# A differential attention block: row maxima taken 1024 columns at a time, scores issued in pairs

## The reference, cut to what matters

```python
B, T, _ = x.shape                        # 4, 1024
q = apply_rope((x @ Wq).reshape(B, T, 32, 8))
k = apply_rope((x @ Wk).reshape(B, T, 16, 8))
v = (x @ Wv).reshape(B, T, 8, 2, 8)
...
def causal_attn(q, k, v, scale):
    s = jnp.einsum('bthd,bshd->bhts', q, k) * scale
    s = jnp.where(mask[None, None], s, jnp.finfo(s.dtype).min)
    p = jax.nn.softmax(s, axis=-1)
    return jnp.einsum('bhts,bshd->bthd', p, v)
attn = causal_attn(q1, k1, vcat, scale) - lambda_full * causal_attn(q2, k2, vcat, scale)
```

## Time and profile before

| | |
|---|---|
| median of 3 runs | 2000.56 us (1993.98 to 2002.34) |
| the profiled execution, span | 2000.2 us |
| PE busy | 1869.5 us, 93% |
| DVE busy | 1456.6 us, 73% |
| ACT busy | 1050.9 us, 53% |
| POOL busy | 670.8 us, 34% |
| first maximum to last value product | 123.3 to 1205.3 us |

### The profile page before, as it was taken

The page is one execution under the profiler, slowest core; times in us unless marked ns, Lnnn a source line. Parts: engine busy times, 40 slices in busy tenths (PEclk is TensorE's granted clock), DMA queues, the critical chain, the costliest instruction groups (busy, mean ns, idle before and its releaser), DMA issues. The chain is left out here.

```text
span 2000.2 us, 42093 instructions
## 1 busy us (share of the span) xinstructions
PE 1869.5 (93%) x11851; PEld 1116.7 (56%) x11851; DVE 1456.6 (73%) x3474; ACT 1050.9 (53%) x2538; POOL 670.8 (34%) x730
## 2 busy tenths in 40 slices
PE   7888999999999999999999999999899999999985
PEld 4543434444343444434444347777688888788874
DVE  7898888988888888888888854444367865433347
ACT  3325567676676666666666644344333323344445
POOL 4542441111111232322223213777703443133324
PEclk9877899999999999999999999999999999999998
DMA  4443342212222121212212102443322211354247
GB/s 129 138 144 103 99 114 71 71 25 71 59 63 80 46 62 40 65 41 59 55 45 62 42 15 85 124 124 111 111 74 88 74 51 54 111 170 141 86 159 150
DMA packets 196455, 170.42 MB, mean 85 GB/s; under 512 B 92120, under 2 KB 176392, under 8 KB 195976
## 3 DMA queue, kind: packets, MB, share of 16 engines
q1 hardware_dynamic: 173064, 115.75, 20.9%
q0 software_dynamic: 20128, 50.35, 8.0%
q10 hardware_dynamic: 3168, 3.15, 0.6%
HBM read 104.16 MB, written 76.90 MB: 91 GB/s over the span
## 5 line engine op out<-in xcount | busy, mean ns | idle before, releaser
L1768 DVE TENSOR_REDUCE mx<-ps 128x1 f32<-128x512 f32 (+3 forms) x1536 | 763.4, 549 | 106.1 <-PE ps L889 85.5
L1358 ACT ACTIVATE fbuf<-ps 128x512 f32<-128x512 f32 (+3 forms) x1024 | 459.4, 507 | 255.6 <-PE ps L900 251.3
L885 PE MATMUL ps<-rbuf 72*128 72x512 bf16 (+3 forms) x1536 | 505.2, 336 | 32.8 <-DVE mx L1768 19.9
L900 PE MATMUL ps<-rbuf 75*128 75x512 bf16 (+3 forms) x1536 | 500.8, 333 | 21.1 <-DMA rbuf<-mrows 18.3
L900 PEld LDWEIGHTS ps<-rbuf 75*128 75x128 bf16 x1536 | 150.3, 98 | 328.0 <-ACT fbuf L1358 138.0
L1358 ACT ACTIVATE gbuf<-ps 128x512 f32<-128x512 f32 (+2 forms) x512 | 211.3, 469 | 102.0 <-PE ps L900 100.9
L732 POOL TENSOR_SCALAR_AFFINE_SELECT gbuf<-gbuf 128x512 f32<-128x512 f32 x96 | 61.4, 640 | 530.3 <-ACT gbuf L1358 530.3
L885 PEld LDWEIGHTS ps<-rbuf 72*128 72x128 bf16 x1536 | 151.9, 99 | 146.3 <-DVE mx L1768 102.9
L915 PE MATMUL ps<-fbuf 128*32 128x512 f32 (+3 forms) x2048 | 228.8, 519 | 2.1 <-issue 0.2
L889 PE MATMUL ps<-maskq,identb 128*128 128x128 bf16 x1024 | 230.1, 225 | 0.0
L739 POOL DMA_INDIRECT y_scr<-wstage,bidx x138 | 138.8, 1006 | 242.2 <-ACT wstage L1402 218.9
(11 more groups left out here) (271 smaller groups left out, 2961.4 us busy)
## 6 DMA issues: line engine op xcount, KB each, us to landing
rbuf<-q_scr SPq DMA_DIRECT2D x192, 96.0 KB
xs_scr<-in_pad SPq DMA_DIRECT2D x8, 1360.0 KB, 6.4
gbuf<-xs_scr SPq DMA_DIRECT2D x69, 136.0 KB, 2.2
gbuf<-xe_scr SPq DMA_DIRECT2D x69, 136.0 KB, 2.1
rbuf<-k_scr SPq DMA_DIRECT2D x192, 48.0 KB
gbuf<-y_scr SPq DMA_DIRECT2D x8, 1024.0 KB, 5.3
q_scr<-gbuf SPq DMA_DIRECT2D x48, 128.0 KB
gbuf<-a_scr SPq DMA_DIRECT2D x12, 512.0 KB, 4.7
```

Source lines behind the costliest of these rows:

```text
L885: ins = pe.matmul(o, qst[par][0:PROWS, i // 4, m, P * (i % 4):P * (i % 4 + 1)], kst[par][0:PROWS, m % 2, 512 * piece:512 * piece + width], ...
L900: pe.matmul(o, kst[par][0:SROWS, m % 2, P * j:P * (j + 1)], qst[par][0:SROWS, h, m, t0:C], start=True, stop=True).then_inc(b_scores, 1)
L1358: act.activation(prob(s)[:, t0:C], ps[:, s % SRING, t0:C], ACT.Exp, scale=SCALE).then_inc(b_exp, 1)
L1768: dve.tensor_reduce(mx[:, i // 4, piece, n:n + 1], ps[:, SRING + s % SRING, 0:width], AX, ALU.max, negate=True).then_inc(b_maxed, 1)
```

## The change: what it does

Maxima: a unit's 48 reductions of up to 512 columns become 18 of 1024 columns, each over a pair of banks. Four kinds of slot fill two banks: "diag" (two query blocks' diagonal pieces of all four maps, behind two mask additions of 512 columns), "one" (one block of queries, 512 keys, two maps), "two" (256 keys, four maps), "four" (128 keys, four maps, two blocks). Two pairs of banks, 3-4 and 5-6, take turns; the transpositions of shift rows and of outputs and the routing's ranks take a slot in the same turn (`ORDER`, 22 slots). The values go to bank 7. A second small reduction (`mfull`) joins a half's maxima. All maxima of a unit are now made within the unit before it (`slot(u, ...)` makes those of u + 1).

Scores: two jobs are issued with one wait and one signal (`b_scores` counts pairs); the exponentials still count jobs. 24 steps t take the place of 48 jobs; steps 7 and 23 have no slot. Values follow every second step, two groups back as before.

SP: a half's three q loads go ahead of its three k loads, with their own semaphores in the second half; the second half's shift rows are stored ahead of the wait for v's place. The routing's ranks are copied to SBUF.

The core of the diff:

```diff
-MAXJ = [(i, 0, m) for i in range(4) for m in range(MAPS)] + \
-       [(i, p, m) for i in range(4, 8) for p in range(2) for m in range(MAPS)]
+REPS = MAPS // 2
+PAIRS = JOBS // 2
+MAXJ = [("diag", 0, 0), ("diag", 0, 2), ("two", 2, 0), ("two", 3, 0), ("four", 0, 1)] + \
+       [("one", i, r) for i in range(4, 8) for r in range(REPS)] + \
+       [("diag", 1, 0), ("diag", 1, 2), ("two", 6, 512), ("two", 7, 512), ("four", 1, 1)]
+MAXA, MAXK = 5, 5 + 4 * REPS
+ORDER = [0, 1, SHIFT_B, 2, 3, 4, 5, OT_B, 6, 7, 8, SHIFT_A, 9, 10, 11, OT_A, 12, 13, 14, 15, 16, 17]
+STEP_OF = [k + (k >= 7) for k in range(len(ORDER))]
...
-LEAD = 43
-LAG = 2 * MAPS
+LAG = 2
...
             def load_qk(u, par, reuse=None):
+                if reuse is not None:
+                    sp.wait_ge(b_scores, PAIRS * reuse - (PAIRS - 2 * LATE))
+                load_q(u, par, 0, b_qk_in[par])
+                load_k(u, par, 0, b_qk_in[par])
+                if reuse is not None:
+                    sp.wait_ge(b_scores, PAIRS * reuse)
+                load_q(u, par, 1, b_q_in[par])
+                load_k(u, par, 1, b_k_in[par])
...
+            def max_matmuls(u, par, w, bank):
+                kind, i, at = MAXJ[w]
+                if w == 0:
+                    pe.wait_ge(b_qk_in[par], 96 * (u // 2 + 1))
...
+                if kind == "diag":
+                    for s in range(2):
+                        pe.matmul(ps[:, bank + s, :].rearrange("p (g w) -> p g w", g=4), identb[:, :],
+                                  maskq[:, :].unsqueeze(1).broadcast_to((P, 4, P)), start=True, stop=False)
+                    for r in range(REPS):
+                        for d in range(2):
+                            for s in range(2):
+                                q = 4 * i + at + d
+                                last = piece(s, r, 2 * P * s + P * d, q, r, P * q, P, False, s == d == 1)
+                elif kind == "one":
+                    for s in range(2):
+                        last = piece(s, s, 0, i, at, 0, C)
...
-                if not (first and s < SRING):
-                    pe.wait_ge(b_exp, JOBS * u + s + 1 - SRING)
+                if not (first and t == 0):
+                    pe.wait_ge(b_exp, JOBS * u + 2 * t - 1)
                 t0 = max(0, P * j - C * h)
-                o = ps[:, ST + s % SRING, t0:C]
-                pe.matmul(o, kst[par][0:SROWS, m % 2, P * j:P * (j + 1)], qst[par][0:SROWS, h, m, t0:C],
-                          start=True, stop=True).then_inc(b_scores, 1)
+                for s in range(2):
+                    last = pe.matmul(ps[:, (2 * t + s) % SRING, t0:C], kst[par][0:SROWS, s, P * j:P * (j + 1)],
+                                     qst[par][0:SROWS, h, 2 * r + s, t0:C], start=True, stop=True)
+                last.then_inc(b_scores, 1)
...
             def unit(u, par, first, last):
+                for t in range(PAIRS):
+                    scores(u, par, t, first)
+                    if not last and t in STEP_OF:
+                        slot(u, par, STEP_OF.index(t), first)
...
+                    if t % REPS == REPS - 1:
+                        g = t // REPS
+                        if g >= LAG:
+                            values(u, par, g - LAG, first)
...
-                    act.wait_ge(b_scores, JOBS * u + s + 1)
+                    if m % 2 == 0:
+                        act.wait_ge(b_scores, PAIRS * u + s // 2 + 1)
...
+                dve.tensor_reduce(to, of, AX, ALU.max, negate=True).then_inc(b_maxed, 1)
+                if w in (MAXA - 1, MAXS - 1):
...
+                    dve.tensor_reduce(mfull[:, h], mx[:, h].rearrange("p c n -> p n c"), AX, ALU.min
+                                      ).then_inc(b_mfull, 1)
```

More of the change, by code:

```diff
@@ L322, in build @@
         TR = 7
+        MX, TAIL = SRING, 6
         def set_ones(eng, par):
@@ L445, in unit @@
                     load_qk(u + 1, 1 - par, None if first else u)
+                store_shift(u, par, 1)
+                if not last:
                     if not first:
@@ L895, in scores @@
+            def scores(u, par, t, first):
+                (h, j), r = GROUPS[t // REPS], t % REPS
+                if t in (0, 4 * REPS):
                     pe.wait_ge(b_shift_in[par][h], 48 * (u // 2 + 1))
-                if not (first and s < SRING):
-                    pe.wait_ge(b_exp, JOBS * u + s + 1 - SRING)
+                if not (first and t == 0):
+                    pe.wait_ge(b_exp, JOBS * u + 2 * t - 1)
                 t0 = max(0, P * j - C * h)
-                o = ps[:, ST + s % SRING, t0:C]
@@ L912, in values @@
                 else:
-                    pe.wait_ge(b_exp, JOBS * u + s + 1)
+                    pe.wait_ge(b_exp, JOBS * u + MAPS * (g + 1))
                 t0 = max(0, P * j - C * h)
[L915 to L923, removed]
@@ L925, in turn_ot, with turn_shift @@
-            def turn_ot(u, h):
+                for m in range(MAPS):
+                    pe.matmul(ps[32 * m:32 * m + 32, OT, t0:C], vu[:, par, j, :], prob(MAPS * g + m)[:, t0:C],
+                              start=(j == 0), stop=(j == 4 * h + 3)).then_inc(b_pv, 1)
+            def turn_shift(u, h, bank):
+                pe.wait_ge(b_mfull, 2 * u + h + 1)
+                pe.transpose(ps[0:16, bank, 0:P], mfull[:, h], ident[:, :]).then_inc(b_mturned, 1)
+            def turn_ot(u, h, bank):
@@ L926, in turn_ot @@
                 pe.wait_ge(b_ot_out, 2 * u + h + 1)
                 for k in range(TB):
-                    ins = pe.transpose(ps[:, TR, k * P:(k + 1) * P], otsb[:, k * P:(k + 1) * P], ident[:, :])
+                    ins = pe.transpose(ps[:, bank, k * P:(k + 1) * P], otsb[:, k * P:(k + 1) * P], ident[:, :])
                 ins.then_inc(b_ot_turned, 1)
-            def unit(u, par, first, last):
[L932 to L949, removed]
-                        pe.wait_ge(b_mrows, 2 * u + 2)
-                        turn_ot(u - 1, 1)
-                    if s == OT_A_AT:
-                        if first:
-                            pe.wait_ge(b_mrows, 2)
-                            pe.wait_ge(r_read, 1)
@@ new lines, in slot @@
+            def slot(u, par, k, first):
+                what, bank = ORDER[k], MX + 2 * ((k + 1) % 2)
+                slot_free(u, k)
+                if what == SHIFT_B:
+                    turn_shift(u, 1, bank)
+                elif what == SHIFT_A:
+                    turn_shift(u + 1, 0, bank)
+                elif what == OT_B:
+                    if first:
+                        rank(bank)
+                    else:
+                        turn_ot(u - 1, 1, bank)
+                elif what == OT_A:
+                    turn_ot(u, 0, bank)
+                else:
+                    max_matmuls(u + 1, 1 - par, what, bank)
@@ L967, in unit @@
+                    if t % REPS == REPS - 1:
+                        g = t // REPS
+                        if g >= LAG:
+                            values(u, par, g - LAG, first)
+                        elif not first:
+                            values(u - 1, 1 - par, len(GROUPS) + g - LAG, False)
+                    if last and t in FOLD_AT:
+                        e = FOLD_AT.index(t)
                         if e < NE:
```

284 lines of the change are left out of this document (161 added, 123 removed).

## The result

The changed kernel takes **2153.5 us** (median of 4, 2140.5 to 2168.5) against 2001.5 for the kernel before in the same batch: a ratio of 1.077 [1.072, 1.083]. The forecast was slower, 2097 us with a range to 2147, so the direction was right and the time lies 6.5 us past the range. The profiled execution has a span of 2146.7 us, 146.5 more than before.

A forecast was written before the change was run, and what follows sets the result against it. PE was taken as the bound, 29.3 of 31.5 us a unit. Pair waits in units 1 to 30 (+75), late first loads (+18) and the ends (+3, +1) sum to +97 on 2000.2: 2097 us, range 2050 to 2147.

The forecast's parts named there:

- The pair's wait: PE before every second score pair: chain through ACT 0.96 us against a slot of 0.44; twelve pauses, 4.6 us a unit.
- The regular term: Units 1 to 30: each becomes 34.0 us, 2.5 more than before, together +75 us.
- PE's floor: PE's streaming work per unit, scores, maxima, values and turns: 29.3 us, unchanged by the packing.
- For DVE the step: Vector engine in a unit: PE's waits for it go, and it is busy some 25 of 34 us.
- Weight loads: Narrow 128-column matmuls on PE: taken at 0.06 us each; rival at 0.098 each gives 2137 us, chance 0.10.
- it lands ... 2.3 late, 1.9 more than now: 15 us in all: First loads on SP in eight units behind a pad store: PE waits 1.9 us more in each, 15 us together.
- the high end: Top of the range, 2147 us: adds weight loads (40) and a clock fall behind some late loads (10).
- the fourth rival: PE's clock: new pauses drop it to 0.50 once a unit, 68 us more, 2165 us; chance 0.07.
- The ends: Outside units 1 to 30: last unit +3 us, packed reductions ahead of unit 0 +1; unit 0 waits about 2.5 more.

The follow-up runs named there:

- either edit alone: Packed kernel with early loads, scores sharing only the wait for two jobs, 1999.4 us, or only the signal, 2021.2 us.
- loads held: Packed kernel with early loads and single scores, seven units' first loads held until job 43 of the unit before: 2009.7 us.

## Why the prediction was wrong

Loads late or on time, pairs or single scores, all with packed maxima (us):

| | pairs | single |
|---|---|---|
| loads of the change | 2153.5 | 2050.7 |
| loads on time | 2112.6 | 1957.7 |

- **The pair's wait: right.** 33.71 us against 34.0, each pause within 0.05 and all twelve 4.3 us against 4.6; ACT is the releaser, and taking both halves away takes 3.59 us a unit away. The regular term was +66 for a forecast of +75.
- **PE's floor: right.** With no pairs a unit is 30.12, of which two late second scores make up 0.7 by starts, so 29.4 for a forecast of 29.3; the 33.71 less 4.3 of pauses gives the same. For DVE the step was right: 26.3 busy us a unit (forecast 25), and never the releaser in the regular unit.
- **Weight loads: right to leave out.** Eight narrow matmuls take 0.50 us.
- **The step that failed** is "it lands ... 2.3 late, 1.9 more than now: 15 us in all". The lateness was right (1.81 to 2.32 us in five units and 3.75 and 4.22 in two; only unit 1 of the eight waited for nothing), its price was not: I charged the wait, and for the clock only the high end's "a fall of the clock behind some late loads (10)". The earlier trace rows showed the half clock behind the wait of 2.14 us, and I took it as a rival about pauses instead of adding it to the late loads. What this term measured is 62 us, not 15, falls in mid-unit included; the seven waits by themselves are 18. The 6.8 us that the kernel before shows behind such a wait would have been too small a price as well: the packed order made them up to 37.5.
- **The argument against the fourth rival was too weak.** It said that several waits a unit ran at 1.00 and the new pauses are under 0.9 us. With loads on time the pauses did bring the clock down in 12 of 28 units, in nine of them for 10.2 us, some 4.3 us each. The argument held for pairs in the order of before, where the longest pause was 0.44 us and not 0.66 by the modelled ends. The Trainium skill (TensorE: Matmul & The Clock Gate, A second HAM failure mode: psum-queue depth-cycling) says that short idles between groups of matmuls over PSUM banks, taken often enough, make the clock oscillate; the trace agrees for pairs with both edits in the packed order (half-clock stretches of 10.2 us) and does not for either edit alone, or for pairs in the order of before (1.00 in the regular units).
- **The ends** cost 18.0 us for a forecast of 6.5: unit 0 8.6 (2.5), the last unit 9.2 (3), the prologue 0.2 (1). No run took them apart, but the clock is in them too: in unit 0 the wait for k was 2.57 us, as forecast, and the clock was at half for 40.0 us in place of 23.6; the last unit, 6.3 longer up to its last value product, has 6.8 us at half clock where it had none.

The time would lie inside the range with either the late loads or the ends as forecast; both sums left the clock out.

Open: why the half clock behind a wait for k mostly lasts longer in the packed order. The place of the wait, or the order of the slots around it, has a part in it; the rest was not found.

## What to carry

Before two operations share a wait or a signal, add up the chain from the first one's start to the moment its buffer is free again, and compare it with the other work between: here 0.96 us against 0.44 cost 3.6 us a unit and hid what the packing had won, until the two were separated. Price a late transfer with the clock that follows it: look in the trace of before for a wait of that length, read the granted clock behind it, and expect that it may last longer in another order. Loads issued ahead of the stores on their queue were worth 41 us with pairs and 93 without in the packed kernel, and nothing in the kernel before.

## What the runs showed of the hardware that I had not expected

A wait of PE of 1.5 to 2.3 us was followed by a granted clock of 0.50 for anything from 0 to 37.5 us, with PE busy for 36.1 of the 37.5; in the packed order with loads held, the same wait at the same place gave 13.7 us five times in a row. Pauses of up to 0.8 us at every second pair brought it down in 12 of 28 units, each time some 17 us from the unit's start, behind the longest pause; shortened by leaving out half of the pair's edit they never did, in 30 units.
